# Moving waits and issues at the borders of two router phases and of a mixer phase

## The reference

```python
x = x + attention0(gate(x, f, w, u, cond))          # delta rule
x = x + router0(gate2(x, f, w, u, cond))            # 64 experts, 6 of them per token
x = x + mixer1(gate3(x, f, w, u, cond))             # in, convolution matrix, out
x = x + router1(gate4(x, f, w, u, cond))            # 8 experts, 2 per token

gate:   tf = sigmoid(sum(cond)); decay = exp(-exp(w)) * (0.5 + 0.5 * tf)
        forward and backward scans over time of exp(f) * f and of exp(f), then
        sigmoid(x) * numerator / denominator * (0.8 + 0.2 * tf)
router: scores = sigmoid or softmax(x @ router); w = top experts' shares, normed, else 0
        out = sum over experts of w[token, expert] * square(relu(x @ w1[expert])) @ w2[expert]
        (+ a shared expert in router0, without shares)
mixer:  out = ((x @ Win) @ Wconv * D * silu(z)) @ Wout
```

## Time and profile before

| what | value |
|---|---|
| median of 3 runs | 1499.11 us (1499.1 to 1503.28) |
| profiled execution, its own time | 1496.33 us |
| span from its first to its last instruction | 1494.5 us |
| PE busy in the span | 1406.2 us (94%) |
| DVE, ACT, POOL busy | 1076.0, 846.8, 382.9 us |
| mean granted clock of TensorE | 0.989 |
| router 0, from its first matmul | 1047.65 us |
| mixer, from its first matmul | 1300.20 us |
| router 1, from its first matmul | 1371.30 us |

### The profile page before, as it was taken

How to read it: one execution, slowest core, us unless ns; L and a number is a source line. 1 busy time by engine, 2 the same in 40 slices (tenths; PEclk the granted TensorE clock), 3 DMA queues, 4 the chain that set the end, 5 groups by cost and what they waited for, 6 DMA issues and landing times.

```text
span 1494.5 us, 23092 instructions
## 1 busy us (share of the span) xinstructions
PE 1406.2 (94%) x8400; PEld 801.6 (54%) x8400; DVE 1076.0 (72%) x2483; ACT 846.8 (57%) x1739; POOL 382.9 (26%) x319
## 2 busy tenths in 40 slices
PE   0989999999999999999999999998899999899998
PEld 0545754755765575575475566575444444344443
DVE  8898888889788888888988978865577567623000
ACT  4567667667577667666766767755533333212432
POOL 4311231050150132113105014015053344100332
PEclk9989999999999999999999999989999999999999
DMA  3000000010010000000001000002283444100220
GB/s 105 15 29 16 22 29 15 2 50 1 16 33 17 17 21 29 16 18 32 16 2 50 1 16 21 1 16 91 71 222 104 107 126 113 56 1 0 71 99 28
DMA packets 21512, 63.41 MB, mean 42 GB/s; under 512 B 4440, under 2 KB 7768, under 8 KB 20256
## 3 DMA queue, kind: packets, MB, share of 16 engines
q1 hardware_dynamic: 19648, 59.25, 12.7%
q10 hardware_dynamic: 1760, 2.76, 0.7%
HBM read 59.61 MB, written 2.39 MB: 41 GB/s over the span
## 4 chain that ended last, share of the span: by engine, by line
PE 82%; DVE 11%; ACT 3%; DMA 1%; issue 1%; POOL 1%; ACTq 0%; SPq 0%; DVEq 0%; POOLq 0%
PE bank L488 13%; PE bank L1759 11%; PE bank L1737 11%; PE bank L525 7%; PE bank L566 7%; PE bank L1858 5%; PE bank L603 4%; PE bank L618 3%; DVE conv L1067 3%; PE bank L535 3%; PE bank L517 3%; PE bank L598 2%; ACT z L883 2%; PE bank L609 2%; PE bank L620 2%; PE bank L510 2%
## 5 line engine op out<-in xcount | busy, mean ns | idle before, releaser
L1067 DVE SCALAR_TENSOR_TENSOR conv<-bank,taps,conv 128x510 f32<-128x510 f32 (+2 forms) x384 | 284.0, 744 | 27.6 <-ACT conv L814 17.9
L488 PE MATMUL bank<-rT,wf 128*128 128x512 f32 x512 | 254.5, 612 | 2.3 <-DVE rT L250 1.4
L1611 POOL TENSOR_TENSOR ffn_weighted<-ffn_relu,ffn_wide 128x512 f32<-128x512 f32 x96 | 125.1, 1335 | 318.2 <-DMA ffn_wide<-ffn_shares 160.4
L1759 PE MATMUL bank<-ffn_weighted,feat 128*128 128x512 f32 x400 | 188.9, 601 | 8.1 <-POOL ffn_weighted L1611 8.1
L1737 PE MATMUL bank<-rT,feat 128*128 128x512 f32 x400 | 186.8, 593 | 0.0
L1622 ACT ACTIVATE ffn_relu<-bank 128x512 f32<-128x512 f32 x100 | 59.7, 597 | 195.1 <-PE bank L1737 195.1
L1301 POOL TENSOR_TENSOR sq<-sq,qsq 128x512 f32<-128x512 f32 x64 | 82.9, 1296 | 277.7 <-ACT sq L993 275.9
L488 PEld LDWEIGHTS bank<-rT,wf 128*128 128x128 f32 x512 | 89.7, 191 | 82.2 <-issue 72.6
L1759 PEld LDWEIGHTS bank<-ffn_weighted,feat 128*128 128x128 f32 x400 | 76.6, 192 | 105.5 <-issue 102.8
L1737 PEld LDWEIGHTS bank<-rT,feat 128*128 128x128 f32 x400 | 76.0, 191 | 93.7 <-issue 93.7
L525 PE MATMUL bank<-zs,wo 128*128 128x512 f32 x256 | 120.8, 603 | 0.0
(11 more groups left out here) (252 smaller groups left out, 2710.6 us busy)
## 6 DMA issues: line engine op xcount, KB each, us to landing
ffn_wide<-ffn_shares SPq DMA_DIRECT2D x64, 256.0 KB, 5.2
feat<-in_L_chunks_dram SPq DMA_DIRECT2D x25, 512.0 KB, 3.5
wf<-in_wf_dram SPq DMA_DIRECT2D x8, 1024.0 KB, 4.8
wz<-in_wz_dram SPq DMA_DIRECT2D x8, 512.0 KB, 3.2
wo<-in_wo_dram SPq DMA_DIRECT2D x8, 512.0 KB, 3.3
ffn_wide<-ffn_shares SPq DMA_DIRECT2D x8, 512.0 KB, 4.4
m<-in_fT_dram SPq DMA_DIRECT2D x2, 512.0 KB, 4.7
xT<-in_xT_dram SPq DMA_DIRECT2D x1, 1024.0 KB, 8.7
```

Of the source, the lines that this page charges most:

```text
L488: ins = pe.matmul(banks[bank_of(p, n)][:], wf[:, c, ORDER[n // NH], :], rT[:, c, halves(n % NH)], start=(c == 0), stop=(c == CT - 1))
L1067: dve.scalar_tensor_tensor(acc[:, :, k:], src[:, :, 0:T - k], taps[:, ORDER[n // NH], KS - 1 - k:KS - k], acc[:, :, k:], ALU.mult, ALU.add ...
L1611: pool.tensor_tensor(hw[:, j, u, :], h2[:, j, u, :], wide[:, j, u // NH % BLOCKS, halves(u % NH)], ALU.mult).then_inc(weighted, 1)
L1759: last = pe.matmul(banks[4 + 2 * c + h][:], chunk[:, slot, CT + t, c * P:(c + 1) * P], of, start=start, stop=stop, skip_group_check=True)
```

## The change

It has five parts. (1) In router 0 PE's transposes of the shares stand one unit earlier, between the first layers of units 2 and 3 of chunk 0, and go to banks 0 and 1 instead of 2 and 3; ACT's copies move likewise, ahead of relu and square of unit 3. In router 1 the transposes stand ahead of the first layer of unit 0 of chunk 1 instead of behind it. (2) POOL waits for the shares of each block apart: `wide_in` has one semaphore for each slot and block, and the wait stands ahead of units 0 and 2. (3) The four DMAs of the mixer's weights are issued by SP, behind the shares of chunks 0 and 1 and the load of chunk 4's weights, instead of by ACT. (4) In the loop ACT takes exp k between the two chunks of pair k, not behind both. (5) Three semaphores of the late gates' factors become one with three steps.

```diff
 def late_gates
-        dve.wait_ge(tf_ready, 1)
-        dve.wait_ge(dw_ready, 1)
+        dve.wait_ge(factor_step, DW)
 moe_phase
-    WIDE = 16 * BLOCKS * ROWS
+    WIDE = 16 * ROWS
-    TURNED = (2, 3) if which == 0 else (4, 5)
+    TURNED = (0, 1) if which == 0 else (4, 5)
-    wide_in = [named(f"wide_in{slot}") for slot in range(2)]
+    wide_in = [[named(f"wide_in{slot}{t}") for t in range(BLOCKS)] for slot in range(2)]
 sync, in follow()
-                                 .partition_broadcast(P // ROWS)).then_inc(wide_in[slot % 2], 16)
+                                 .partition_broadcast(P // ROWS)).then_inc(wide_in[slot % 2][t], 16)
 sync, behind follow() of chunks 0 and 1
+        if which == 0:
+            ahead_of(sp)
 gpsimd
+                    if u % NH == 0 and u // NH < BLOCKS:
+                        pool.wait_ge(wide_in[j][u // NH], k * WIDE + WIDE)
                     if u == 0:
-                        pool.wait_ge(wide_in[j], k * WIDE + WIDE)
 scalar
-            units(0, 0)
+            for u in range(UNITS - 1):
+                unit(SHARED + u, 0, u, h2)
 (here stand the copies of the transposed shares)
+        if which == 0:
+            units(0, 0, UNITS - 1)
         units(1, 1)
         if late:
-            ahead_of(act)
             late["exp"](act, 0)
         with act.Fori(1, NW // 2) as k:
-            for j in range(2):
-                units(k * 2 + j, j)
+            units(k * 2, 0)
             if late:
                 late["exp"](act, k)
+            units(k * 2 + 1, 1)
 tensor
-            for u in range(UNITS):
+            for u in range(UNITS - 1):
                 opened(0, u)
                 if u < 2:
                     shared(u + 2)
         else:
             for u in range(2, UNITS):
                 opened(0, u)
-            opened(1, 0)
         pe.wait_ge(w_ready, 1)
         if which == 0:
-            pe.wait_ge(relu_done, SHARED + UNITS)
+            pe.wait_ge(relu_done, SHARED + 2)
 (here stand the transposes)
-        for u in range(1 - FIRST, UNITS):
-            if which == 0 and u == TURNED[0]:
-                pe.wait_ge(wT_ready, NH)
+        if which == 0:
+            opened(0, UNITS - 1)
+            pe.wait_ge(wT_ready, NH)
+        for u in range(UNITS):
             opened(1, u)
```

More of the change, by code:

```diff
@@ L1399, in late_gates @@
     nf, df, nb, db = (sb(n, [P, G, T]) for n in ("fwd_num", "fwd_den", "bwd_num", "bwd_den"))
-    side_in, tsum_ready, tf_ready, ew_ready, dw_ready, ex_ready, exp_done, step_done = (
-        named("late_" + n) for n in ("side_in", "tsum_ready", "tf_ready", "ew_ready", "dw_ready", "ex_ready",
-                                     "exp_done", "dve_step"))
+    side_in, tsum_ready, factor_step, ex_ready, exp_done, step_done = (
+        named("late_" + n) for n in ("side_in", "tsum_ready", "factor_step", "ex_ready", "exp_done", "dve_step"))
+    TF, EW, DW = 1, 2, 3
     BEFORE_SLICES, SLICE_STEPS = 2, 13
@@ L1412, in scalar @@
         act.wait_ge(tsum_ready, 1)
[L1413 to L1416, removed]
+        act.activation(tf[:], tsum[:], ACT.Sigmoid).then_inc(factor_step, 1)
+        act.activation(ew[:], wu[:, G:2 * G, :], ACT.Exp).then_inc(factor_step, 1)
+        act.wait_ge(factor_step, EW)
+        act.activation(dw[:], ew[:], ACT.Exp, scale=-1.0).then_inc(factor_step, 1)
     def exp(act, k):
@@ L1570, in open_sync, with sync @@
             sp.dma_start(gate, env["gate_dram"]).then_inc(gate_in, 16)
-    def sync(sp):
+    def sync(sp, ahead_of=None):
         def follow(c, slot, more):
@@ L1616, in gpsimd, with scalar @@
             pair(k)
-    def scalar(act, ahead_of=None):
+    def scalar(act):
         def unit(n, j, u, to):
@@ L1624, in unit, with units @@
             act.activation(to[:, j, u, :], h2[:, j, u, :], ACT.Square).then_inc(square_done, 1)
-        def units(c, j):
-            for u in range(UNITS):
+        def units(c, j, first=0):
+            for u in range(first, UNITS):
                 unit(SHARED + c * UNITS + u, j, u, h2)
@@ L1971, in _ @@
             for n in range(LAST):
-                parts[n]["sync"](sp)
+                if n == 1:
+                    parts[1]["sync"](sp, parts[2]["weights_in"])
+                else:
+                    parts[n]["sync"](sp)
                 if n == 0:
@@ L1997, in _ @@
             for n in range(LAST):
-                if n == 1:
-                    parts[1]["scalar"](act, parts[2]["weights_in"])
-                else:
-                    parts[n]["scalar"](act)
+                parts[n]["scalar"](act)
                 arrive(act)
```

## The result

The changed kernel takes 1484.92 us in the median of 4 runs (1483.82 to 1485.98), the kernel before 1499.16 us beside it (1499.1 to 1503.28). The ratio is 0.9901, with a 95% interval from 0.9884 to 0.9918, so it is faster by 14.2 us. The forecast was 1484.6 us. The profiled execution took 1484.96 us, its span is 1483.2 us, 11.3 us less than the span of the profile before (1494.5 us); why these two differences are not the same stands with the account of the prediction.

A forecast was written before the change was run, and what follows sets the result against it. PE, busy 94% of the span, was taken as the bound, so only its standing still counts. Gaps 10.9 us, mixer restart 2.0 and one further restart 1.6 gave 14.5 us off, 1484.6 us by the median; eight in ten 1480.5 to 1490.

The forecast's parts named there:

- The thin room of 0.1 us for PE's new wait: Router 0's opening: copies end at 1072.70, PE's first layer of unit 3 about 1072.9, so PE's wait finds them done.
- 4.05 forecast: Router 0's opening: 1.86 us from earlier copies plus 2.19 us from waiting by blocks, leaving a gap of 1.93 us.
- Part 3 at nothing: Mixer's weights on SP: chunk 2's shares still land before PE needs them, so the part is costed at nothing.
- my two bounds: Landing of chunk 2's shares behind the weights on SP: 1093 or 1108.9, middle 1101; needed by 1107.8.
- the rival's 1.1 us: Turn 2 of router 0's loop: chunk 2's shares land late behind the weights, 1.1 us lost, 1486 us; chance 0.05.
- 5.95 and 2.01 us: Border to the mixer: PE's gap of 6.47 us shrinks to 0.5, gaining 5.95; the slow restart of 2.01 goes too.
- One fast of two: Restarts behind the remaining gaps of 1.93 and 1.96 us in routers 0 and 1: evens each, likeliest one fast, 1.6 us.
- the argument by two neighbouring lengths: Gaps of 1.93 and 1.96 us lie between 1.40 us, which left the clock high, and 2.19 us, followed by the lower level.
- the sum: Whole kernel: 10.9 us of gaps, 2.0 for the mixer's restart and 1.6 for one other restart, gain 14.5 us.
- the 2.8 us by which the profile before lay under its median: Profiled execution forecast at 1481.8 us; as it lies 2.8 us under the median of runs, the median forecast is 1484.6.

The follow-up runs named there:

- weights_by_act: The changed kernel with part 3 undone: ACT issues the mixer's weights ahead of exp 0; 1485.46 us, ratio 0.9907 to the kernel before.
- exps_behind_pair: The changed kernel with part 4 undone: ACT takes exp k behind both chunks of pair k; 1491.16 us, ratio 0.9951 to the kernel before.
- before_exps_between: The kernel before with part 4 alone: exp k between the two chunks of pair k; 1492.72 us, ratio 0.9953 to the kernel before.
- turn_later_r1: The changed kernel with part 1 undone in router 1: transposes behind unit 0 of chunk 1; 1486.53 us, beside 1484.27 for the changed kernel.
- after_again: The changed kernel timed once more, nothing altered; 1484.27 us, ratio 0.9905 to the kernel before.
- wide_logits: The changed kernel with router 1's logits as matmuls of 128 x 64 instead of 128 x 8; 1483.17 us, ratio 0.9895 to the kernel before.

## Why the prediction was right, step by step

- **Part 1, router 0.** Forecast: copies at 1071.62, POOL and PE 1.86 us earlier. Measured: copies at 1072.68, 1071.54 on the clock of before; undoing it costs 2.12 us. The thin room of 0.1 us for PE's new wait held: its 20 records abut. That undoing gives 0.26 us more than the forecast is of the size of the scatter of the openings.
- **Part 2.** Forecast: 2.19 us from the landing of the second DMA, 4.1 us after its issue. Measured: 4.10 us after its issue, and undoing it costs 2.36 us in the opening. Together the opening is 3.94 us shorter, against 4.05 forecast; the gap is 2.13 against 1.93, since the write of the shares took 3.16 us instead of 2.97.
- **Part 3 at nothing.** Right in time: the loop has no gap. The shares of chunk 2 were down at 1100, 1098.9 on the clock of before, near the middle of my two bounds (1101) and nearer to the lower one (1093) than to the upper (1108.9). The rule that I took from the Trainium skill (page "DMA: Bandwidth & Descriptors", section "Queues, rings and completion order") agrees with the traces in direction: the shares behind the weights take 10.0 us instead of 8.0, and 3 MB more ahead moved them by 7.8 us. What I made of it was wrong, that the upper bound is then the nearer one: that bound took the 19.7 us of `mixer_wout` over from a queue of its own, and in SP's it was 12.2. So the rival's 1.1 us didn't come. That the part buys nothing is less sure than the result: weights_by_act shows no stop only behind a slow restart.
- **Part 4.** Forecast 5.95 and 2.01 us. Measured by the stretches: loop 0 is 7.48 us shorter, of which the fast restart behind the opening is 1.6, so 5.9; mixer 1.93. Exp 1 came at 1106.5 on the clock of before (forecast 1105.8), ACT stood and PE didn't. exps_behind_pair and before_exps_between show the cause from both sides.
- **Part 1, router 1.** 0.93 us forecast, 0.9 shown by the gap of turn_later_r1. In the changed kernel's profile the gap was 2.06 us for 1.96, but the opening as a whole grew by 0.85 us, for the reason below.
- **Restarts.** One fast of two was forecast, at evens, and that is what the first profile has. But evens were too kind, and the argument by two neighbouring lengths was weak. Over all profiles gaps of 1.68 to 1.83 us had a fast restart in four of four, those from 1.95 to 2.39 us a slow one in ten of twelve; then 2.68 and 3.38 us had a fast one, and 2.88, 2.89, 4.49, 5.20 and 5.67 a slow one. A restart costs 1.6 to 2.4 us or nothing, and the gap's length alone doesn't tell which.
- **What the sum left out.** The clock can fall in router 1's opening. It did in the profile after (3.49 us for the first layer, 1.6 us) and not in that of before. From profile to profile the sum gave 14.5 us and 11.3 were measured: of the 3.2 missing, 1.8 are opening 1 (0.85 longer for 0.93 shorter), 1.14 the clock in the phase ahead of router 0, and the rest tenths. The median came out at the forecast all the same, since the prediction took the 2.8 us by which the profile before lay under its median as holding for the changed kernel too, and there the profile lies at the median (1484.96 and 1484.92). Two errors of 3.2 and 2.8 us cancel, and that is luck: the places and sizes of the gaps were forecast rightly, the 0.3 us of the total was not earned. Where the other runs of the kernel before lost time was not profiled; of its 32 executions beside the experiments 12 have the profile's mean granted clock of 0.989 and 20 a lower one, from 0.985 to 0.987.

## What to carry to other kernels

Read where a background job's input is issued, not only how long the job takes: one exponential behind two chunks instead of one set the end of a gate, and with it a gap of 6.5 us and a slow restart. Where a first consumer waits for a transfer, let it wait for its own piece, and make that piece small: here by blocks it was worth over 2 us, by halves another 2 us and the slow restart. Price a gap of TensorE at its length plus what the restart costs, in these profiles nothing or 1.6 to 2.4 us, and give chances for the second part, since gaps of equal length went either way (2.13 us was followed by a fast one and by a slow one). Before a forecast from one profile is carried to a median, ask whether that profile's distance from its median will be the same in the changed kernel.

## What was not expected of the hardware

The granted clock fell in router 1's opening in 8 of the 12 profiles in which its logits are matmuls of 128 x 8, though PE had stood for only 0.26 us ahead of them. This costs about 1.6 us where one first layer was slow and some 5 us where it lasted on (opening 1: 21.8 to 26.3 us; at the high clock 18.8 to 21.3, by the kernel). With logits of 128 x 64, which take the same time (1.97 us for 16 records, 1.92 with 128 x 8), it fell in neither of two profiles, and in none of 14 in router 0's opening, which always has them. The runs point the same way: they spread by 2.9 us in after_again and by 0.4 us in wide_logits, by 5.3 us with shares by halves alone and by 1.1 us with the wider logits added, whose four executions all have a mean granted clock of 0.993 where the others' have 0.989 to 0.993. That it comes from these small matmuls is thus likely and not shown: with a fall in two of three profiles, two without one would come about by chance in one case of nine, the kernels compared were timed in different rounds, and no run tells what else at this border takes part.
